# Layer 2's odd 96 rows computed as layer 1's, in a two-layer fp32 kernel on one core

## What is computed

```python
# layer 1, x: 1024 x 512, S = 128, F = 1248, G = 6
approx_up = x @ up_w.T;  delta = x @ gate_w.T - local_point
approx_out = approx_up @ local_approx_output.T + sum_m (delta^m / m! * approx_up) @ fuse_weight_m.T
ffn_out = silu(x @ ffn_gate_w.T) * (x @ ffn_up_w.T) @ ffn_down_w.T
x = layernorm(x + approx_out + ffn_out)
# layer 2, H = 1376: w1, w2 (H x 512) and w3 (512 x H) are first rounded to 16 levels
# per block of 64 weights, scaled by the block's largest magnitude
dq = CODE[searchsorted(bounds, w / absmax)] * absmax
x = layernorm(x + (silu(x @ dq1.T) * (x @ dq2.T)) @ dq3.T)
```

## Time and profile before

| | us |
|---|---|
| median of three runs | 410.64 |
| the profiled execution's own time | 410.27 |
| its span, first to last instruction | 408.2 |
| PE busy | 399.9 (98%) |
| DVE busy | 324.3 (79%) |
| POOL busy | 289.8 (71%) |
| ACT busy | 267.0 (65%) |

### The profile page before, as it was taken

The page is one execution under the profiler, slowest core; times in us unless marked ns, Lnnn a source line. Parts: engine busy times, 40 slices in busy tenths (PEclk is TensorE's granted clock), DMA queues, the critical chain, the costliest instruction groups (busy, mean ns, idle before and its releaser), DMA issues.

```text
span 408.2 us, 5342 instructions
## 1 busy us (share of the span) xinstructions
PE 399.9 (98%) x1762; PEld 325.8 (80%) x1762; DVE 324.3 (79%) x385; ACT 267.0 (65%) x372; POOL 289.8 (71%) x228
## 2 busy tenths in 40 slices
PE   8999999999999999999999999999999999999993
PEld 6767888888888888888888888888888877888872
DVE  4539889789889996999969799887789989925035
ACT  5574676686685847466955668887769777732613
POOL 0177998986978499737992465799999998954330
PEclk9999999999999999999999999999999999999998
DMA  8993111000104362003052000000000000000202
GB/s 276 406 408 126 53 22 51 28 26 0 53 20 116 92 213 71 26 0 104 1 167 112 0 2 0 0 2 0 2 2 0 2 0 0 2 1 0 104 0 103
DMA packets 10010, 26.42 MB, mean 65 GB/s; under 512 B 1248, under 2 KB 1632, under 8 KB 9728
## 3 DMA queue, kind: packets, MB, share of 16 engines
q1 hardware_dynamic: 9552, 25.30, 17.9%
q10 hardware_dynamic: 432, 0.79, 0.7%
HBM read 23.99 MB, written 2.10 MB: 64 GB/s over the span
## 4 chain that ended last, share of the span: by engine, by line
PE 95%; DVE 1%; POOL 1%; ACT 1%; issue 0%; POOLq 0%; DVEq 0%; ACTq 0%
PE PS L1292 31%; PE PS L1294 31%; PE PS L1293 31%; PE PS L1426 1%; PE PS L1330 1%; PE PS L1420 1%; POOL level L1217 1%; DVE h L917 0%; POOLq L262 0%; PE PS L1435 0%; DVE PS L885 0%; ACT side L635 0%; ACT side L597 0%; PE PS L1438 0%; PE PS L1441 0%
## 5 line engine op out<-in xcount | busy, mean ns | idle before, releaser
L1217 POOL TENSOR_SCALAR level<-side 128x1024 f32<-128x1024 int8 (+2 forms) x119 | 129.0, 1084 | 27.7 <-ACT side L597 15.4
L885 DVE TENSOR_TENSOR PS<-PS,level 128x1024 f32<-128x1024 f32 (+2 forms) x102 | 120.1, 1178 | 22.6 <-POOL level L1217 18.8
L1292 PE MATMUL PS<-x_hi,w_hi 128*128 128x512 f32 (+1 forms) x340 | 132.7, 390 | 0.3 <-DVE h L917 0.3
L1294 PE MATMUL PS<-x_hi,w_lo 128*128 128x512 f32 (+1 forms) x340 | 132.4, 389 | 0.0
L1293 PE MATMUL PS<-x_lo,w_hi 128*128 128x512 f32 (+1 forms) x340 | 132.3, 389 | 0.0
L597 ACT ACTIVATE side<-Q 128x1024 int8<-128x1024 f32 (+2 forms) x84 | 80.6, 998 | 22.1 <-DVE PS L881 18.0
L1247 POOL TENSOR_TENSOR l_lo<-h,l_hi 128x512 fp32r<-128x512 f32 (+1 forms) x42 | 57.3, 1374 | 26.5 <-ACT l_hi L597 25.8
L1292 PEld LDWEIGHTS PS<-x_hi,w_hi 128*128 128x128 f32 (+1 forms) x340 | 63.4, 186 | 15.1 <-issue 0.8
L1294 PEld LDWEIGHTS PS<-x_hi,w_lo 128*128 128x128 f32 (+1 forms) x340 | 63.4, 186 | 13.8
L1293 PEld LDWEIGHTS PS<-x_lo,w_hi 128*128 128x128 f32 (+1 forms) x340 | 63.4, 186 | 13.6
L1293 PE MATMUL PS<-x_lo,l_hi 128*128 128x512 f32 (+1 forms) x144 | 56.1, 389 | 0.0
(11 more groups left out here) (103 smaller groups left out, 515.2 us busy)
## 6 DMA issues: line engine op xcount, KB each, us to landing
Q<-w SPq DMA_DIRECT2D x10, 512.0 KB, 13.9
raw<-w_in SPq DMA_DIRECT2D x9, 512.0 KB, 9.9
raw<-w_out SPq DMA_DIRECT2D x13, 256.0 KB, 2.7
raw<-w SPq DMA_DIRECT2D x5, 512.0 KB, 3.9
R<-xN SPq DMA_DIRECT2D x2, 1024.0 KB, 6.4
raw<-w_fuse SPq DMA_DIRECT2D x7, 256.0 KB, 2.5
out<-R SPq DMA_DIRECT2D x7, 256.0 KB, 2.0
h<-xT SPq DMA_DIRECT2D x2, 512.0 KB, 7.0
```

The source lines that it names most:

```text
L885: v.tensor_tensor(total, total, level_of(s), ALU.add).then_inc(s_add, 1)
L1217: g.tensor_scalar(level_of(s), side_of(s), LIMITS[k][1], LIMITS[k][0], ALU.min, ALU.max).then_inc(s_level, 1)
L1292: t_.matmul(dst, a_hi, b_hi, start=start, stop=False)
L1294: return t_.matmul(dst, a_lo, b_hi, start=False, stop=stop)
```

## The change

**The odd chunk.** Chunk 10 of layer 2 is moved to position 4, so it runs as pairs 8 and 9; chunks 4 to 9 follow at positions 5 to 10. It is packed as chunk 0 of layer 1 is: 12 matmuls a pair for 96 gate and 32 up rows, and in pair 8 also eight plain fp32 matmuls for the 64 up rows left of both halves (`project_up2`). These write bank 3, which pair 7 uses, so PE waits for `bank_free(7)` ahead of them. ACT's `silu` for pairs 8 and 9 copies the up in two parts.

**Its operands.** Plain fp32 needs x whole, and layer 2 has it only as high and low parts. POOL adds them in four instructions of 128 x 2 x 512 (`join_x`), one ahead of each of `gate_times_up(2)` to `gate_times_up(5)`, into a part of `h` that is free then. `split_nf4(4)` copies the 64 up rows whole and the rest as the high part.

**Units.** Unit 4 is now 128x768, and unit 10 is 128x1024.

**The floor.** `amax` lies in every second element of `floored`, and the others hold the constant TINY. The floor is a `tensor_reduce` with max over each pair of elements, where it was a `tensor_scalar`. w3's floor L868 stays.

**SHARE.** From unit 8 on some steps are dealt to other calls: POOL clamps u10k3 before `gate_times_up(5)`, and from call 11 to 14 it does one or two more clamps ahead of the multiplication than before, which call 15 does less. In the second stage DVE does lo_w3(1) and lo_w3(2) one add or transpose earlier, and ACT spreads its last draws.

```diff
+ODD = 4
+CHUNK_OF = [*range(ODD), C2 - 1, *range(ODD, C2 - 1)]
@@ ACT, silu
+                    if is_odd(layer, i):
+                        for to, up_rows in parted_up(layer, i):
+                            last = copy(up2[to, k % 2, :], up_rows)
+                        last.then_inc(s_up2, 1)
@@ DVE, scales
-                v.tensor_scalar(inverse, maxima, TINY, None, ALU.max).then_inc(s_floor, 1)
+                v.tensor_reduce(inverse, pairs, AX_X, ALU.max).then_inc(s_floor, 1)
@@ POOL
+            def join_x(half, k):
+                pool.wait_ge(s_xl, X_PARTS + TILES * (half + 1))
+                x, hi, lo = (t[:, 2 * k:2 * k + 2, half * HALF:(half + 1) * HALF] for t in (x2_raw, x_hi, x_lo))
+                g.tensor_tensor(x, hi.bitcast(F32), lo.bitcast(F32), ALU.add).then_inc(s_x2raw, 1)
...
             for i in range(2 * C2):
+                if 2 <= i < 6:
+                    join_x(i // 2 - 1, i % 2)
                 if on_pool(i):
                     gate_times_up(i)
@@ PE
+            def project_up2():
+                w = up2_raw.rearrange("p s (k m) -> p k s m", k=2)
+                for c in range(DC):
+                    pe.wait_ge(s_x2raw, 3 + c // 2)
+                    for half in range(2):
+                        last = t_.matmul(PS[half * LEFT:(half + 1) * LEFT, UP_BANK[2], :], w[:, c // 2, c % 2, :],
+                                         x2_raw[:, c, half * HALF:(half + 1) * HALF], start=c == 0, stop=c == DC - 1)
...
+                if is_odd(layer, i):
+                    last = project_odd(layer, slot, half, bank)
+                    if layer == 2 and half == 0:
+                        pe.wait_ge(*bank_free(i - 1))
+                        last = project_up2()
```

More of the change, by code:

```diff
@@ L44 @@
 REST, LEFT = F1 % P, 64
-assert 2 * REST - P == LEFT
+assert F2 % P == REST and 2 * REST - P == LEFT
+ODD = 4
+CHUNK_OF = [*range(ODD), C2 - 1, *range(ODD, C2 - 1)]
 KEEP_FROM = 5
@@ L304, in turned, with odd_part @@
             return PS[:, XT_BANK:XT_BANK + 2, :].rearrange("p b n -> p (b n)")[:, 0:unit_width(f)]
+        x2_raw = h[:, 6 * TOK:(6 + DC) * TOK].rearrange("p (c t) -> p c t", c=DC)
+        up2_raw = h[:, 5 * TOK:5 * TOK + DC * LEFT].rearrange("p (s n) -> p s n", s=2)
+        def odd_part(w, first, last):
+            return w.rearrange("p (s n) -> p s n", s=2)[:, :, first:last]
         def term_tile(m, a):
@@ L440, in h_half @@
             view = h[0:job_rows(SEQ[n][1]), c * TOK + a * HALF:c * TOK + (a + 1) * HALF]
[L441 removed]
+            return view, (s_h, 2 * c + a + 1) if layer == 1 else product_made(PAIR2[CHUNK_OF.index(c), a])
         def product_made(i):
@@ L715, in split_nf4 @@
                 beside()
-                m = rows(f, F2)
                 act.wait_ge(s_turn, f + 1)
                 wait_nf4_slot(act, f)
-                copy(in_slot(w_hi, f, 2 * DC * m), turned(f)).then_inc(s_whi4, 1)
+                dst = in_slot(w_hi, f, unit_width(f))
+                if f == ODD:
+                    copy(up2_raw, odd_part(turned(f), 2 * P, 2 * (P + LEFT)))
+                    copy(odd_part(dst, 0, 2 * P), odd_part(turned(f), 0, 2 * P)).then_inc(s_whi4, 1)
+                else:
+                    copy(dst, turned(f)).then_inc(s_whi4, 1)
             def split_w3(c):
@@ L914, in gate_times_up @@
                 dve.wait_ge(s_silu, i + 1 + (2 * C1 if layer == 2 else 0))
-                if layer == 1 and i < 2:
-                    for to, up_rows in parted_up(i):
+                if is_odd(layer, i):
+                    for to, up_rows in parted_up(layer, i):
                         last = v.tensor_tensor(dst[to, :], up_rows, dst[to, :], ALU.mult)
@@ L1329, in project_up @@
                     for half in range(2):
-                        last = t_.matmul(PS[half * LEFT:(half + 1) * LEFT, UP_BANK, :], w[:, c, :],
+                        last = t_.matmul(PS[half * LEFT:(half + 1) * LEFT, UP_BANK[1], :], w[:, c, :],
                                          xT_raw[:, c, half * HALF:(half + 1) * HALF], start=c == 0, stop=c == DC - 1)
@@ L1335, in pair @@
                 f, half, bank = pair_of(layer, i)
-                m = rows1(f) if layer == 1 else rows(f, F2)
+                m = P
                 if layer == 1:
@@ L1357, in pair @@
                     pe.wait_ge(s_xl, X_PARTS + (TILES if half == 0 and i < 2 else TT))
-                if layer == 1 and i < 2:
-                    last = project_first(half, bank)
-                    if half == 0:
+                if is_odd(layer, i):
+                    last = project_odd(layer, slot, half, bank)
+                    if layer == 2 and half == 0:
+                        pe.wait_ge(*bank_free(i - 1))
+                        last = project_up2()
+                    elif half == 0:
                         last = project_up()
@@ L1509, in by_squares @@
         parts = []
-        for f in range(C2):
+        for f in CHUNK_OF:
             rows_ = [w[f * P:(f + 1) * P].reshape(-1, SQ, 2, DC, BLOCK) for w in ws]
+            if f == C2 - 1:
+                gate, up = rows_
+                parts += [x.transpose(3, 1, 2, 0, 4).reshape(P, -1)
+                          for x in (np.concatenate([gate, up[LEFT // SQ:]]), up[:LEFT // SQ])]
+                continue
             parts.append(np.stack(rows_).transpose(4, 2, 0, 3, 1, 5).reshape(P, -1))
```

58 lines of the change are left out of this document (38 added, 20 removed), and 12 rows, old and new, of the table SHARE.

## The result

| | before | after |
|---|---|---|
| median of five runs, in turn on one chip | 410.58 us (409.98 to 410.75) | 413.33 us (412.8 to 413.63) |
| the profiled execution's own time | 410.27 | 412.80 |
| its span | 408.2 | 410.8 |
| PE busy | 399.9 | 398.9 |
| POOL busy | 289.8 | 299.6 |

The ratio of after to before is 1.0063, with a 95% interval of 1.0051 to 1.0075. The change makes the kernel slower by 2.75 us. The forecast was 413.1.

What follows compares the result with a forecast made beforehand. PE was taken as the bound, POOL as a second just ahead of it. 410.27 + 3.1 (L 6.0 less margin 2.9) = 413.4, put at 413.1 us for collisions partly missed; own range 411.5 to 414.2, 8 in 10 408.4 to 414.6.

Steps and rivals of the forecast that it cites:

- The bound: Whole kernel: PE, busy 98% of the span, sets the time; POOL, without idle time from 262 to 342 us, is second.
- L: On POOL in layer 2: the time by which it reaches the same clamp later than before, forecast 6.0 us.
- PE's saving: At the odd chunk: 24 matmuls and eight plain fp32 ones replace 48 matmuls, a gain of 1.8 us.
- POOL's debt: POOL before 262 us: joins 9.9, unit 10 1.9, less 8.6 idle, plus collisions 1.7 and a wait 1.1: 6.0 us.
- collision: DVE's first add of a unit beside POOL's work: costs a working POOL 0.86 us, once a unit, + 1.7 us together.
- Pair 4: PE at pair 4, whose low parts come behind DVE's delayed add: a wait of 0 to 0.3 us.
- Pair 8: PE ahead of pair 8's fp32 matmuls: stands still 3.6 us for the copy of pair 7, ending at 270.8 us.
- Pair 10: Low parts of units 5 to 10: margins of 4.9 us or more, so they don't set the end.
- The second stage sets the end: At w3's chunk 3: PE's end moves by L less a margin of 2.9 us, 6.0 - 2.9 = + 3.1 us.
- The old deal: Order of steps before the change: margin 2.2 us at chunk 3; the new order takes out one 0.7 us transpose, giving 2.9.
- The rest: Floor, ACT's second copies, DMA and moved draws: cost nothing; the floor - 1.3 to + 0.2 us of DVE's time.
- Rival 1: The saving stays: needs L under 1.1 us, PE's waits stay at zero, 408.5 us; chance 0.25.

Runs made afterwards that it cites:

- e1: The changed kernel without its four joins and without PE's wait for them, part of the output left out; 409.43 us, ratio 0.9971.
- e2: The changed kernel with two joins ahead of unit 9's division and the other two ahead of pairs 2 and 3; 412.25 us, ratio 1.0043.
- e5: The changed kernel with two joins behind unit 9's clamps, ahead of POOL's first layer 2 multiplication, the others ahead of pairs 2 and 3; 412.11 us.
- e6: The changed kernel with two joins behind unit 9's clamps and the other two one pair later, ahead of multiplications 3 and 4; 412.47 us.
- e9: The changed kernel with two joins waiting for DVE's last small norm steps, the other two ahead of multiplications 3 and 4; 409.83 us, ratio 0.9985.
- e10: e9 with three steps dealt anew: DVE's u11k1 and u15k4 adds later, POOL's u15k6 and u15k7 clamps ahead of multiplication 20; 410.3 us, ratio 0.9997.

## Why the prediction was right, point by point

**The bound.** Right. With the joins gone, 1.83 us of L leave a gain of 0.9 us; with them, 5.17 us turn it around.

**PE's saving.** Right. The fp32 matmuls took 3.59 us from their start to the next matmul, as in layer 1 (23.31 - 19.73 = 3.58); the forecast's 3.67 holds the 0.09 ahead of them too. Without the wait, in e1, it is 271.42 - 267.52 - 0.23 = 3.67 again.

**POOL's debt.** The mechanism was right, the size a little too large: L = 6.0 forecast, 5.17 measured (5.4 without the early offset). The joins took 2.38 to 2.41 us each (2.40). POOL's work ahead of the end of u10k2's clamp was 259.57 - 235.48 = 24.1 us (24.4). One collision cost POOL 0.86 us as assumed. The other, at the multiplication of 238.50, cost 1.61 - 1.29 = 0.32, because POOL had come 0.64 us too early for ACT anyway. Unit 11's division was forecast for 265.7 and came at 264.67, after a wait of 1.48 us for DVE's inverse, as before. Of that 1.0 us, 0.4 is that the first join began at 235.48 and not at 235.9, 0.3 is POOL's sum, and 0.3 is DVE's path behind it.

**Pair 4.** No pause (0 to 0.3 forecast).

**Pair 8.** The wait came where and why it was forecast, 2.82 us instead of 3.6. The copy of pair 7 ended at 269.78, not at 270.8: the same 1.0 us by which the division was early.

**Pair 10.** Missed: PE paused 0.83 us there. The step that failed is the sentence that the low parts of units 5 to 10 had margins of 4.9 us or more and so didn't set the end. I held them against L alone. The low parts of unit 5 ended at 270.60 us in the kernel before and end at 277.00 in after, 6.4 us later. That is 5.4 us by which DVE's scaling of unit 10 starts later (272.49 against 267.08), 2.02 - 1.29 = 0.73 for the first add of unit 11, which now meets POOL at work, and 1.23 - 0.96 = 0.27 for the scaling of the full unit 10. PE, 0.9 us late by then, had 4.8 + 0.9 us to give. A margin must be held against L plus what DVE itself loses on the way.

**The second stage sets the end.** This was the term that carried the forecast, L less a margin of 2.9 us. Six kernels have the new deal of steps at pair 17 and after, and a pause at chunk 3 that comes from DVE's steps there:

| kernel | pair 17's multiplication on POOL | first matmul of chunk 3 | between |
|---|---|---|---|
| after | 330.64 | 351.58 | 20.94 |
| e1, no joins | 327.30 | 348.27 | 20.97 |
| e2, joins early | 329.81 | 350.77 | 20.96 |
| e5, gap, then pairs 2 and 3 | 329.84 | 350.80 | 20.96 |
| e6, gap, then pairs 3 and 4 | 330.26 | 351.22 | 20.96 |
| e9, after the norm | 327.94 | 348.88 | 20.94 |

The distance is the same in all six within 0.03 us, whatever pauses PE had had before. Five of the six could be read another way: they all pause at pair 10, and from its first matmul to that of chunk 3 they take 74.47 to 74.50 us each, so pair 10 might be what decides. Two kernels speak against that. e1 has no pause at pair 10 (74.00 us from there to chunk 3) and keeps the 20.97; and in e10 the pause at pair 10 is gone and chunk 3 starts no earlier. So chunk 3 starts when POOL's queue, and DVE's behind it, allow it. The kernel before had 349.18 - 325.47 = 23.71 there: a margin of 23.71 - 20.95 = 2.76 us (2.9 forecast). For after this gives 5.17 - 2.76 = + 2.4 us, and chunk 3 is 2.40 late; given the constant distance this has to come out so. The test is the time: the restart costs 0.13 us more, and the two profiled executions are 2.53 us apart. For e9 it gives - 0.3 and for e1 - 0.9, where the profiled executions are 0.04 and 0.8 us faster and the medians 0.6 and 0.9 us. The pauses at pairs 8 and 10 and at chunk 0 only take in advance what chunk 3 would have taken. With 6.0 - 2.9 = 3.1 the forecast was 0.7 too late in this term; I had taken 0.3 off for collisions that might be missed, and the medians lie 0.2 us further apart than the two profiled executions. The forecast also started from the profiled execution, 0.3 us under the median of 410.58. That it ended 0.2 us from the result is in part luck: the term was too large, and these three go the other way.

**The old deal.** With it the forecast's margin was 2.2 us. The joins alone gave 3.61 - 2.2 = 1.4 (1.6 measured), the fills 1.17 us of L and no loss, and the old deal in the changed kernel 7.22 - 2.2 = 5.0 (5.3 measured). The sums agree within 0.3 us, or 0.8 with the early offsets taken off, though PE's last pauses in the first and the third of these kernels are for ACT's copies and not for DVE, so the place is not shown. What the new deal is worth was underrated: it also spares POOL the 2.27 us of waiting for a draw, and L is 7.22 - 5.17 = 2.05 us less with it, 1.25 with the early offsets taken off. With the transpose of 0.7 us that is 2.0 of the 2.5 us; the rest stays open.

**The rest.** The floor costs nothing, as forecast. Rival 1, that the saving stays, needed L under 1.1 or a free place for the joins. For two of the four e9 has such a place, and it brings back a part of the saving, not all of it. My accounts of POOL's idle time before 236 us had left it out, because I looked only at the stretch where the change had put them.

**Open.** e9 keeps a pause of 0.44 us at pair 10 and 0.36 at chunk 0. Whether a version without debt at pair 17 would give the full 1.86 us wasn't tried.

## What to carry to other kernels

In this kernel an engine with no idle time just behind the bound was a second bound. Where you find one, sum what it gets until its next long wait, subtract the idle time it has, and compare the rest with the margin at the last place where it meets the bound; earlier pauses are not added to that. Each margin is to be held against the debt plus the collisions on the other engines of that chain. An idle stretch of GpSimd isn't free if VectorE runs small steps on the critical chain beside it (here 2.3 us between two kernels): place long reads behind the last of them. And a lateness that is read from two traces needs a zero: read it also at a place ahead of the change.

## What was not expected of the hardware

**Two elements, 1.8 us.** A VectorE `tensor_scalar` of 128x2 took 1.82 us beside a join of POOL, 0.17 without; a `tensor_tensor` of that size took 1.12 us, and 0.16 without.

**TensorE's clock after a pause.** In the profiled execution with the draws moved (415.74 us; the median is 414.15), PE stood still for 3.6 us ahead of pair 10. The windows of that kernel, with the granted clock in the third column from the end:

```profile
264.00:274.00 10.00, 10.00 (x45) 6.12 (x44) 9.14 (x9) 7.46 (x10) 8.12 (x8) 1.00 0.00 0
278.00:284.00 6.00, 5.83 (x14) 4.60 (x15) 4.91 (x5) 5.94 (x9) 5.75 (x5) 0.50 0.01 3
284.00:294.00 10.00, 10.00 (x45) 8.25 (x44) 7.95 (x7) 7.46 (x11) 9.51 (x9) 0.99 0.00 0
```

The granted clock is 0.50 behind the pause, the 1.2 GHz level, and matmuls start 0.43 us apart; in the stretches around it is the 2.4 GHz level. From 278.17 to 284.22 us there are 14 of them, 6.05 us where 14 x 0.227 = 3.18 would do: 2.9 us more, on top of the pause. After the 2.82 us pause of the changed kernel the profiled execution has the full clock. The record has only a mean granted clock for the other five executions of the kernel with the draws moved: all six lie between 0.987 and 0.991, where the 23 of the kernel before beside it have 0.995 to 0.998. So all six were at the lower level for some time, and the 414.15 us hold it, which is where the 0.8 us above the changed kernel can come from. Why one pause was followed by the lower level and the other not, these runs don't show.
